# A graph network kernel whose work between the two passes over the edges is cut into chunks of four tiles and dealt out anew to ScalarE, GpSimd and VectorE

## The chip, the cores and the metric

The kernel runs on one core of one Trainium2 chip. The metric is the device time of one execution in microseconds (us), lower is better. The profile's span is the time from the first to the last instruction of one execution; "its own time" is what that same execution took as the metric counts it.

## What is computed

The reference is a two-layer graph network on 6250 nodes of 96 features and 206250 directed edges, sorted by destination. Cut to what matters:

```python
# layer 0
agg_sum = segment_sum(x[src], dst); deg = segment_sum(1, dst)
out1 = batch_norm(x @ W_self1 + (agg_sum / max(deg, 1)) @ W_neigh1, g1, beta1)
hp = relu(x @ W_pool + b_pool)
out2 = batch_norm(x @ W_self2 + segment_max(hp[src], dst) @ W_neigh2, g2, beta2)
x = layernorm(x + leaky_relu(out1 + out2, 0.01))
# layer 1: Q, K, V = x @ W + b; E = edge_attr @ We + be; 8 heads of 12
w = exp(clip(sum_over_head(K[src] * Q[dst] * E / sqrt(12)), -5, 5))
x = layernorm(x + segment_sum(V[src] * w, dst) / (segment_sum(w, dst) + 1e-6))
```

Batch norm takes its mean and variance over all nodes, so nothing behind it can start before the last edge of layer 0 has been summed. Layer 1 gathers rows of K and V at random, so its first gather needs the whole table of them.

## The kernel before, in words

The edges are taken in 404 groups of 512 (four columns of 128), four groups to a turn, 101 turns. Two passes go over all groups.

**Pass 1** (`turn1` on each engine). GpSimd issues four indirect DMAs for each group, which fetch `x[src]` into `kvg` (L469, `gathers`). TensorE transposes the rows (L1194), applies the pool weights (L1205), sums a window of 64 nodes with one-hot matrices (`sums`, L1237), turns the running maximum back (`back`, L1246) and picks the maxima (`ends`, L1254). VectorE makes the one-hot matrices (L742), scans the running maximum (L759) and adds both windows to `acc` (L769: sums in `acc[:, 0]`, maxima in `acc[:, 1]`). The sums, maxima and the features `xT` lie with features on partitions and nodes on columns. Nodes whose edges are all in are finished on the way, in strips of 62 nodes: one strip each turn, `LATE` = 3 turns behind, its linear layers in steps 1 and 3 of the turn, with the batch norm statistics of each strip (L795). The last 174 nodes (`REST`) come after the loop, in order: count (L1297), maximum, reciprocal and product on VectorE (L880 to L884), linear layers (L1299 to L1304), statistics of the rest (L888), then one aggregation over all 99 entries for each branch (L890), square root (L565) and the five small steps that give scale and shift (L896 to L901). Before them each engine loads a flag and branches on it (`irregular`, for inputs whose edges don't fit the strips; not taken here).

**Between the passes** (`nodes`). The 49 tiles of 128 nodes go in seven chunks of seven tiles. For a chunk of 896 columns: ScalarE scales and shifts branch 2 in place (L572); VectorE adds the scaled branch 1 (L927) and takes the leaky ReLU (L930); GpSimd adds `xT` (L487); TensorE transposes to nodes on partitions (L1327); VectorE takes layer norm statistics (L907, L911); ScalarE the square root (L589); VectorE reciprocal and bias (L917, L919); ScalarE normalizes into `xN` (L593); TensorE transposes back (L1319) and ScalarE copies to `xT` (L577); TensorE multiplies with the K and V weights (L1333); VectorE (L936) and ScalarE (L584) copy the table rows to `stage`; SyncE's queue stores them (L367). The engines run the seven chunks skewed by up to three steps. GpSimd then clears `acc[:, 0]` (L490) and all wait until the table is in HBM.

**Pass 2** (`turn2`). GpSimd gathers table rows (again L469, waits for `s_msg` of four groups before); TensorE transposes the edge features and one-hots (L1348, L1355), multiplies with We and spreads the queries (L1364, L1374, L1383) and sums messages (L1391); VectorE multiplies and reduces (L1001, L1012, L1019, L1036); ScalarE copies and takes the exponential (L621, L623, L631). In step 2 of turn 0 TensorE does three extra matmuls that nobody reads (`stay_warm`, L1310). The last 12 turns are written out, with the output rows of finished nodes.

Each engine executes its own instructions in the order written. Between engines there are only counting semaphores. Three lines that the steps below lean on: the second leaky step of the kernel before, what GpSimd does with its result, and the statistics that wait for TensorE:

```python
L930  dve.scalar_tensor_tensor(out=o2, in0=o1, scalar=0.01, in1=o1, op0=ALU.mult, op1=ALU.max)
L487  pool.tensor_tensor(acc[0:D, 0, at], acc[0:D, 1, at], xT[0:D, at], ALU.add)
L907  dve.bn_stats(lnst[:, k, :], source(k))      # source: a bank of PSUM
```

Of the kernel before, what the change touches and what calls it, by code (L numbers as in the profile page):

```python
# [41 lines left out]
KV_BANKS = (6, 7, 4, 5)  # L42
SW = N // TURNS + 1
LATE = 3
# [16 lines left out]
def build(nc, x, src, dst, src_m, src_t, dst_m, dst_t, prv_m, prv_t, nxt_m, nxt_t, edge_attr, Ws1, Wn1, Wp, bp, Ws2, Wn2,  # L61
          g1, be1, g2, be2, Wq, bq, Wk, bk, We, be, Wv, bv, out):
    ctx = ExitStack()
    with ctx:
# [3 lines left out]
        def sem(name):  # L68
# [54 lines left out]
        limit = sb("limit", [1, NS])  # L123
        share = sb("share", [D, W])
        pick = sb("pick", [DSUM, D])
        mv = sb("mv", [D, 2, 2])
# [6 lines left out]
        small = keep[:, :, :].rearrange("p g j -> p (g j)").bitcast(F32)  # L133
        lnst = small[:, 0:K7 * 6].rearrange("p (k c) -> p k c", k=K7)
# [7 lines left out]
        share_rest = prod[0:D, 1, 0:REST]  # L142
        stats = ea[0:D, :, :, :].rearrange("p r j c -> p (r j c)")[:, 0:2 * (NS + 1) * 6].rearrange(
# [8 lines left out]
        early = sb("early", [1, 1])  # L152
# [37 lines left out]
                                                         sem("s_stat"), sem("s_bn"), sem("s_std"))  # L190
        s_countR, s_shareR, s_meanR, s_linR, s_statR, s_copyR = (
# [7 lines left out]
        s_x1T, s_x1c, s_kv, s_kvD, s_kvA = sem("s_x1T"), sem("s_x1c"), sem("s_kv"), sem("s_kvD"), sem("s_kvA")  # L199
# [44 lines left out]
        def pipeline(eng, turn, lag, turns=TURNS, per=R, peel=0, between=(), unrolled=0):  # L244
# [8 lines left out]
            last = turns - unrolled  # L253
# [3 lines left out]
            for p in range(last, turns):  # L257
                turn(p, range(per), lambda r: True)
            turn(turns, range(lag), lambda r: r < 0)

        def node_rows(t, k):

            return bank[t % 2 * 2 + k // 4][:, (k % 4) * D:(k % 4 + 1) * D]
# [20 lines left out]
        def irregular(eng):  # L284

            return eng.If(load_flag(eng) > 0)

# [13 lines left out]
        LAST = ((DONE, DONE + 3), (DONE + 3, NT))  # L301

# [3 lines left out]
        def _(sp):  # L306
# [30 lines left out]
            for w, v, b in ((w_kv[:, 0:D], Wk, bk), (w_kv[:, D:2 * D], Wv, bv),  # L337
                            (w_q[:, :], Wq, bq), (w_e[:, :], We, be)):
                sp.dma_start(w[0:D, :], v[:, :]).then_inc(s_wb, 16)
                sp.dma_start(w[D:D + 1, :], b.rearrange("(a c) -> a c", a=1)).then_inc(s_wb, 16)  # L340
            with nc.allow_non_contiguous_dma(reason="four columns of 96 numbers"):
# [24 lines left out]
            def store_table(i, k0, k1):  # L366
                sp.dma_start(kv_table[bass.ds(i * KC + k0 * P, (k1 - k0) * P), :].rearrange("(t p) c -> p t c", p=P),  # L367
# [1110 lines left out]
```

## Time and profile before

| | us |
|---|---|
| median of 3 runs | 4170.03 (4162.75 to 4170.11) |
| the profiled execution, its own time | 4178.03 |
| its span | 4176.3 |
| busy: TensorE 3767.2, GpSimd 3075.5, VectorE 2324.7, ScalarE 1511.1 | |
| pass 1 ends with the last window added | at 2042.9 |
| batch norm's scale and shift are ready | at 2054.9 |
| the table is in HBM | at 2122.9 |
| first gather of pass 2 | at 2124.0 |

Times "at" are counted from the span's start. "Busy" is the time an engine executed instructions; matmul ends are modelled. In rows of the timeline the first number is the start, the second how long the merged instructions took from first start to last end, and the bracket tells how long the engine had been idle and what ended that.

### The profile page before, as it was taken

What the parts mean: (1) busy time and instruction counts of PE and PEld (TensorE: products, weight loads), DVE (VectorE), ACT (ScalarE), POOL (GpSimd) and SP (SyncE); (2) the same over time, 40 slices, a digit from 0 to 9 for tenths busy, and PEclk for the clock granted to TensorE, in tenths of its full rate; (3) what the DMA queues carried; (4) which work ended last, traced back from release to release, by engine and by line L of the source; (5) the groups of instructions that cost most, each with busy time, mean ns of one, the idle gap of its engine ahead of it and who ended that gap; (6) DMA issues with size and microseconds to landing.
All of it is one profiled execution on the core that took longest, in us unless ns stands there. A gap on an engine that the chain in (4) does not pass through costs nothing.

```text
span 4176.3 us, 105692 instructions
## 1 busy us (share of the span) xinstructions
PE 3767.2 (90%) x30382; PEld 3261.3 (78%) x30382; DVE 2324.7 (56%) x5943; ACT 1511.1 (36%) x4211; POOL 3075.5 (74%) x3246
## 2 busy tenths in 40 slices
PE   7988888888888888888799999999999999999998
PEld 6777777777777777777688888888888888888887
DVE  6555555555555555555545555555555555555666
ACT  3333333333333333333343333333333333333344
POOL 7777777777777777777457777777777777777775
PEclk9999999999999999999779999999999999999998
DMA  3111111111111111111134444444444444444443
GB/s 93 40 40 39 39 40 39 40 40 39 40 40 39 40 39 39 40 39 40 38 108 120 117 118 118 118 119 118 118 118 119 117 118 118 118 118 118 118 121 94
DMA packets 208705, 331.25 MB, mean 79 GB/s; under 512 B 72877, under 2 KB 156520, under 8 KB 208648
## 3 DMA queue, kind: packets, MB, share of 16 engines
q0 software_dynamic: 129040, 238.05, 23.2%
q1 hardware_dynamic: 79608, 92.48, 7.4%
q8 instruction: 30, 0.49, 0.1%
q14 instruction: 27, 0.22, 0.0%
HBM read 323.08 MB, written 7.22 MB: 79 GB/s over the span
## 4 chain that ended last, share of the span: by engine, by line
POOL 42%; issue 32%; PE 12%; DMA 9%; DVE 4%; POOLq 1%; ACT 0%; DVEq 0%; SPq 0%; ACTq 0%
POOL kvg L469 41%; DMA kvg<-kv_table,idx 7%; DMA kvg<-in_x_dram,idx 2%; PE bank L1355 2%; PE bank L1374 1%; PE bank L1194 1%; PE bank L1364 1%; DVE prod L1012 1%; PE bank L1391 1%; DVE msg L1036 1%; PE bank L1205 1%; PE bank L1237 1%; PE bank L1254 1%; PE bank L1348 1%; PE bank L1333 1%
## 5 line engine op out<-in xcount | busy, mean ns | idle before, releaser
L469 POOL DMA_INDIRECT kvg<-kv_table,idx x1613 | 1526.0, 946 | 516.0 <-issue 472.7
L469 POOL DMA_INDIRECT kvg<-in_x_dram,idx x1613 | 1527.2, 947 | 497.2 <-issue 485.9
L759 DVE TENSOR_TENSOR_SCAN scan<-keepC,scan,bank 96x512 f32<-96x512 bf16 x404 | 515.4, 1276 | 495.0 <-PE bank L1205 493.8
L1194 PE MATMUL bank<-ident,kvg 128*96 128x128 f32 x3232 | 450.6, 283 | 228.4 <-DMA kvg<-in_x_dram,idx 218.1
L1194 PEld LDWEIGHTS bank<-ident,kvg 128*96 128x96 f32 x3232 | 365.3, 163 | 293.1 <-DMA kvg<-in_x_dram,idx 218.7
L1355 PE MATMUL bank<-ident,S 128*64 128x128 f32 x3232 | 438.3, 279 | 126.9 <-DVE S L742 124.7
L1001 DVE TENSOR_TENSOR prod<-kvg,bank 128x384 f32<-128x384 f32 x404 | 223.1, 552 | 532.6 <-DMA kvg<-kv_table,idx 393.7
L1355 PEld LDWEIGHTS bank<-ident,S 128*64 128x64 f32 x3232 | 349.0, 138 | 215.7 <-issue 215.7
L1254 PEld LDWEIGHTS bank<-S,scanE 128*96 128x96 f32 x3232 | 338.3, 165 | 216.7 <-issue 214.9
L548 ACT COPY scanE<-bank 128x384 f32<-128x384 f32 x404 | 193.2, 478 | 750.1 <-PE bank L1246 750.1
L1374 PE MATMUL bank<-qwin,scan 64*128 64x96 f32 x3232 | 461.4, 284 | 0.0
L1364 PE MATMUL bank<-w_e,eaC 97*128 97x96 f32 x3232 | 443.1, 281 | 0.0
L769 DVE TENSOR_TENSOR acc<-acc,bank 97x64 f32 (+1 forms) x808 | 177.6, 220 | 469.0 <-issue 461.9
L742 DVE TENSOR_TENSOR S<-bank,rel 128x512 f32<-128x512 f32 (+1 forms) x808 | 435.5, 539 | 2.4 <-DMA kv_table<-stage 2.4
L1205 PE MATMUL bank<-eaC,w_pool 97*96 97x512 f32 x808 | 429.7, 614 | 0.0
L542 ACT COPY eaC<-bank 96x512 f32<-96x512 f32 x404 | 234.9, 581 | 532.5 <-PE bank L1196 532.5
L1374 PEld LDWEIGHTS bank<-qwin,scan 64*128 64x128 f32 x3232 | 394.5, 189 | 39.6 <-issue 1.2
L1364 PEld LDWEIGHTS bank<-w_e,eaC 97*128 97x128 f32 x3232 | 398.6, 194 | 0.8 <-issue 0.8
L621 ACT COPY eaC<-bank 96x512 f32<-96x512 f32 x404 | 234.9, 581 | 437.9 <-PE bank L1348 434.4
L1391 PE MATMUL bank<-S,msg 128*104 128x64 f32 x3232 | 387.4, 264 | 4.3 <-DVE msg L1036 4.3
L1391 PEld LDWEIGHTS bank<-S,msg 128*104 128x104 f32 x3232 | 331.7, 173 | 53.1 <-DVE msg L1036 4.8
L623 ACT COPY scan<-bank 64x512 f32<-64x512 f32 x404 | 233.6, 578 | 325.5 <-PE bank L1355 316.1
(164 smaller groups left out, 5127.2 us busy)
## 6 DMA issues: line engine op xcount, KB each, us to landing
ea<-in_edge_attr_dram SPq DMA_DIRECT2D x402, 192.0 KB
kvg<-in_x_dram,idx POOLq DMA_INDIRECT x1613, 2.5
kvg<-kv_table,idx POOLq DMA_INDIRECT x1613
kv_table<-stage SPq DMA_DIRECT2D x6, 672.0 KB, 3.3
xN<-in_x_dram SPq DMA_DIRECT2D x6, 336.0 KB, 3.2
out_dram<-stage SPq DMA_DIRECT2D x5, 384.0 KB
src_all<-in_src_groups_dram SPq DMA_DIRECT2D x1, 804.0 KB
stage<-in_dst_groups_dram SPq DMA_DIRECT2D x1, 804.0 KB
```

The lines of the kernel that those rows point to most:

```text
L469: pool.indirect_dma_start(out=to[:, r, j, :], out_offset=None, in_=table, in_offset=bass.IndirectOffsetOnAxis(ap=idx[:, r, j:j + 1], axis= ...
L542: act.copy(xeC[0:D, r % 2, :], bank[0][0:D, :])
L621: act.copy(eaC[0:D, r % 2, :], bank[0][0:D, :]).then_inc(s_ec, 1)
L742: dve.tensor_tensor(S[:, r % R, 0:cols * J, :], iota.unsqueeze(1).to_broadcast([P, cols * J, W]), rel[:, bass.ds(i * R + r, 1), 0:cols, :] ...
L759: dve.tensor_tensor_scan(out=scan[:, r % 2, :], data0=keepC[:, r % 2, :], data1=bank[2 + r % 2][0:D, :], initial=scan[:, (r + 1) % 2, GE - ...
L1194: pe.matmul(bank[0][0:D, j:GE:J], xg[:, r, j, 0:D], ident[:, :], start=True, stop=True)
L1205: pe.matmul(bank[2 + b][0:D, :], w_pool[:, :], xeC[:, b, :], start=True, stop=True).then_inc(s_hpT, 1)
L1254: last = pe.matmul(bank[7][0:D, 0:W], scanE[:, b, j, :], S[:, r % R, J + j, :], start=j == 0, stop=j == J - 1)
L1355: last = pe.matmul(bank[1][0:W, j * P:(j + 1) * P], S[:, r % R, j, :], ident[:, :], start=True, stop=True)
L1364: pe.matmul(bank[2 + b][:, j * D:(j + 1) * D], eaC[:, b, j * P:(j + 1) * P], w_e[:, :], start=True, stop=True)
L1374: last = pe.matmul(bank[4 + b][:, j * D:(j + 1) * D], stC[:, b, j * P:(j + 1) * P], qwin[:, b, :], start=True, stop=True)
L1391: last = pe.matmul(bank[6 + b][0:DMSG, 0:W], msg[:, b, j, :], S[:, r % R, j, :], start=j == 0, stop=j == J - 1)
```

## The change

Pass 1: strips come two turns behind in place of three (`LATE` = 2, so the rest is 112 nodes), with mean in step 1 and the linear layers in steps 2 and 3. After turns 98 and 99 VectorE aggregates the first 96 strips' statistics of one branch each and folds the result into one entry (`gathered_stats`). The rest's count, reciprocal and product move into the drain of the pass, ahead of the last two windows of maxima on VectorE, and the flag is loaded there too. The K and V weights are centred by one matmul (`w_kvc`), so that the table can be made from the value before layer norm, scaled by the row's 1/std and with the bias added.

Between the passes: 13 chunks of four tiles (the last has one). ScalarE scales both branches (two activations), GpSimd adds them, VectorE takes the leaky ReLU in place, GpSimd adds `xT`, TensorE transposes and multiplies with `w_kvc` from the same source, VectorE takes the statistics and writes the table rows as scale and bias, ScalarE normalizes into `xN`. The transposes back, the copies to `xT`, ScalarE's table copies and GpSimd's clear are gone from here.

Pass 2: for the first 12 turns (`HEAD`) each step also transposes one tile of `xN` (TensorE), copies it to `xT` (VectorE) and clears one tile of `acc` (ScalarE). `stay_warm` is gone. The first 12 turns are written out on TensorE.

The diff, cut to its core:

```diff
-LATE = 3
+LATE = 2
+NA = TURNS - LATE - 3
+Q = 4
+NQ = -(-NT // Q)
+HEAD = 12
@@ @block.gpsimd @@
+            for k in range(NQ + 1):
+                if k < NQ:
+                    at = columns(k)
+                    pool.wait_ge(s_l, k + 1)
+                    pool.tensor_tensor(acc[0:D, 1, at], acc[0:D, 0, at], acc[0:D, 1, at], ALU.add).then_inc(s_zs, 1)
+                if k >= 1:
+                    at = columns(k - 1)
+                    pool.wait_ge(s_leak, k)
+                    pool.tensor_tensor(acc[0:D, 0, at], acc[0:D, 1, at], xT[0:D, at], ALU.add).then_inc(s_h, 1)
+            pool.wait_ge(s_kvtab, 16 * NQ)
@@ @block.scalar @@
+            for k in range(NQ + 3):
+                if k < NQ:
+                    at = columns(k)
+                    act.activation(acc[0:D, 0, at], acc[0:D, 0, at], ACT.Identity, bias=shs[:, :], scale=ga[:, 0:1])
+                    act.activation(acc[0:D, 1, at], acc[0:D, 1, at], ACT.Copy, scale=ga[:, 1:2]).then_inc(s_l, 1)
+                if 2 <= k < NQ + 2:
+                    t = k - 2
+                    act.wait_ge(s_mv, t + 1)
+                    act.activation(qr[b][:, 0:n], qmv[b].rearrange("p (n c) -> p n c", c=2)[:, 0:n, 1], ACT.Sqrt,
+                                   bias=eps_col[:, 0:1]).then_inc(s_sd, 1)
+                if k >= 3:
+                    t = k - 3
+                    act.wait_ge(s_nb, t + 1)
+                    for j in tiles_of(t):
+                        last = act.activation(xN[:, t * Q + j, :], bank[2 + b][:, j * D:(j + 1) * D], ACT.Identity,
+                                              bias=qb[b][:, j:j + 1], scale=qr[b][:, j:j + 1])
+                    last.then_inc(s_x1, 1)
@@ @block.scalar, turn2 @@
+                def clear_ahead(r):
+                    if head:
+                        clear(act, bass.ds((i * R + r + 1) * P, P))
...
+                def rest_out():
+                    dve.wait_ge(s_countR, 1)
+                    dve.tensor_scalar_max(share_rest, bank[6][0:D, W:W + REST], 1.0).then_inc(s_shareR, 1)
+                    dve.reciprocal(share_rest, share_rest).then_inc(s_shareR, 1)
+                    dve.tensor_tensor(acc[0:D, 0, rest], acc[0:D, 0, rest], share_rest, ALU.mult).then_inc(s_meanR, 1)
...
+            def gathered_stats(m, done, n):
+                part = stats[:, m, NA - 1, :]
+                dve.bn_aggr(mv[:, m, :], stats[:, m, 0:NA, :].rearrange("p n c -> p (n c)")).then_inc(done, 1)
+                dve.memset(part[:, 3:4], float(NA * SW))
+                dve.tensor_copy(part[:, 4:5], mv[:, m, 0:1])
+                dve.tensor_scalar_mul(part[:, 5:6], mv[:, m, 1:2], float(NA * SW)).then_inc(done, 1)
...
-                step(dve.bn_aggr(mv[:, m, :], stats[:, m, :, :].rearrange("p n c -> p (n c)")))
+                step(dve.bn_aggr(mv[:, m, :], stats[:, m, :, :].rearrange("p n c -> p (n c)")[:, NA * 6 - 3:]))
@@ @block.vector @@
+            for k in range(NQ + 3):
+                if k < NQ:
+                    z = acc[0:D, 1, columns(k)]
+                    dve.wait_ge(s_zs, k + 1)
+                    dve.scalar_tensor_tensor(out=z, in0=z, scalar=0.01, in1=z, op0=ALU.mult, op1=ALU.max
+                                             ).then_inc(s_leak, 1)
+                if 2 <= k < NQ + 2:
+                    t = k - 2
+                    dve.wait_ge(s_hN, t + 1)
+                    wait_past(dve, s_x1, t - 1)
...
+                    last.then_inc(s_mv, 1)
+                if k >= 3:
+                    t = k - 3
+                    dve.wait_ge(s_kv, t + 1)
+                    for j in tiles_of(t):
+                        last = dve.scalar_tensor_tensor(
+                            out=stage[:, t * Q + j, :],
+                            in0=bank[4 + t % 2 * 2 + j // 2][:, j % 2 * 2 * D:(j % 2 + 1) * 2 * D],
+                            scalar=qr[t % 2][:, j:j + 1], in1=b_kv[:, :], op0=ALU.mult, op1=ALU.add)
+                    last.then_inc(s_kvD, 1)
+                if 2 <= k < NQ + 2:
+                    t = k - 2
+                    dve.wait_ge(s_sd, t + 1)
+                    dve.reciprocal(qr[b][:, 0:n], qr[b][:, 0:n]).then_inc(s_rs, 1)
@@ @block.tensor @@
+            for t in range(NQ):
+                pe.wait_ge(s_h, t + 1)
+                wait_past(pe, s_x1, t - 1)
+                for j in tiles_of(t):
+                    last = pe.transpose(bank[2 + b][:, j * D:(j + 1) * D],
+                                        acc[0:D, 0, (t * Q + j) * P:(t * Q + j + 1) * P], ident[0:D, 0:D])
+                last.then_inc(s_hN, 1)
+                wait_past(pe, s_kvD, t - 1)
+                for j in tiles_of(t):
+                    last = pe.matmul(bank[4 + b * 2 + j // 2][:, j % 2 * 2 * D:(j % 2 + 1) * 2 * D],
+                                     acc[0:D, 0, (t * Q + j) * P:(t * Q + j + 1) * P], w_kvc[:, :],
+                                     start=True, stop=True)
+                last.then_inc(s_kv, 1)
...
-                        stay_warm(3, 6)
```

## Rows read from the trace of the kernel before

**Rows 1.** The page, costliest groups: GpSimd's gathers of pass 2 (busy, mean ns, idle before).
```profile
L469 POOL DMA_INDIRECT kvg<-kv_table,idx x1613 | 1526.0, 946 | 516.0 <-issue 472.7
```

**Rows 2.** Stretches: us; busy PE, PEld, DVE, ACT, POOL; clock, DMA share, GB/s.
```profile
2060.00:2096.00 36.00, 28.50 (x113) 25.16 (x113) 24.32 (x93) 20.84 (x51) 11.83 (x6) 0.50 0.17 57
...
2123.00:2142.00 19.00, 18.42 (x74) 15.56 (x75) 4.75 (x13) 4.94 (x11) 13.70 (x15) 0.52 0.37 99
2142.00:2162.00 20.00, 20.00 (x162) 17.49 (x161) 10.00 (x29) 7.02 (x25) 13.72 (x15) 1.00 0.39 108
```

**Rows 3.** Timeline of the end of pass 1 and of the batch norm chain.
```profile
2033.29 0.22 DVE L769 TENSOR_TENSOR acc<-acc,bank 96x64 f32 x1 [0.61 <-issue]
...
2040.35 0.66 PE L1246 MATMUL bank<-ident,scan 96*128 96x96 f32 x4
2040.66 0.22 DVE L769 TENSOR_TENSOR acc<-acc,bank 96x64 f32 x1 [1.72 <-PE bank L1254]
...
2042.68 0.22 DVE L769 TENSOR_TENSOR acc<-acc,bank 96x64 f32 x1 [1.80 <-PE bank L1254]
...
2044.30 0.90 PE L1297 MATMUL bank<-acc,pick 97*96 97x174 f32 x2 [1.77 <-issue]
...
2045.61 1.24 DVE L882 RECIPROCAL prod<-prod 96x174 f32<-96x174 f32 x1
...
2050.75 2.83 DVE L890 BATCH_NORM_AGGREGATE mv<-ea 96x2 f32<-96x594 f32 x1
...
2053.67 0.30 ACT L565 ACTIVATE std<-mv,eps_col 96x2 f32<-96x2 f32 x1 [1.32 <-DVEq L891]
...
2054.96 3.18 ACT L572 ACTIVATE acc<-acc,shs,ga 96x896 f32<-96x896 f32 x3 [0.99 <-DVE shs L901]
```

**Rows 4.** Timeline: TensorE's table matmuls of two chunks in a row.
```profile
2079.65 4.85 PE L1333 MATMUL bank<-w_kv,xT 97*128 97x192 f32 x14
...
2087.75 4.85 PE L1333 MATMUL bank<-w_kv,xT 97*128 97x192 f32 x14
```

**Rows 5.** Groups of instructions by form, 2042 to 2124: busy us, mean ns.
```profile
L593 ACT ACTIVATE xN<-bank,keep 128x96 f32<-128x96 f32 x49 | 16.5, 438 | 3.3 <-DVE keep L919 3.3
...
L930 DVE SCALAR_TENSOR_TENSOR acc<-acc 96x896 f32<-96x896 f32 x7 | 9.4, 1338 | 0.2
...
L907 DVE BATCH_NORM_STATS2 keep<-bank 128x6 f32<-128x96 f32 x49 | 8.7, 248 | 0.6 <-PE bank L1327 0.6
...
L572 ACT ACTIVATE acc<-acc,shs,ga 96x896 f32<-96x896 f32 x7 | 7.7, 1131 | 1.0 <-DVE shs L901 1.0
...
L911 DVE BATCH_NORM_AGGREGATE keep<-keep 128x2 f32<-128x6 f32 x49 | 4.0, 154 | 1.0 <-DVE keep L907 0.2
```

**Rows 6.** Timeline around GpSimd's first addition, and a later one.
```profile
2058.40 1.14 DVE L927 SCALAR_TENSOR_TENSOR acc<-acc,ga 96x896 f32<-96x896 f32 x1
2058.87 2.60 POOL L487 TENSOR_TENSOR acc<-acc,xT  x1 [31.69 <-DVE acc L930]
2059.57 2.84 DVE L930 SCALAR_TENSOR_TENSOR acc<-acc 96x896 f32<-96x896 f32 x1
...
2068.35 2.08 POOL L487 TENSOR_TENSOR acc<-acc,xT  x1 [3.51 <-DVE acc L930]
```

**Rows 7.** The chain's piece to the table's landing, and the first gather's timeline row.
```profile
2120.71 2.21 DMA kv_table<-stage
...
2124.04 0.97 POOL L469 DMA_INDIRECT kvg<-kv_table,idx  x1 [16.77 <-issue]
```

**Rows 8.** First groups of pass 2: two TensorE rounds, the extra matmuls, GpSimd's waits.
```profile
2130.69 1.97 PE L1355 MATMUL bank<-ident,S 128*64 128x128 f32 x8
...
2137.83 1.97 PE L1355 MATMUL bank<-ident,S 128*64 128x128 f32 x8
...
2140.05 3.10 PE L1310 MATMUL bank<-xT,ident 96*128 96x448 f32 x6
...
  DVE msg L1036: 3.9, 7
```

More of the change, by code:

```diff
@@ L838, in _ @@
             dve.wait_ge(s_scan, NG + AHEAD)
-            with irregular(dve):
+            with dve.If(held["flag"] > 0):
                 with dve.Fori(0, NCH) as c:
@@ L1187, in _ @@
             pe.wait_ge(s_rel, 1)
+            rest = slice(NS * SW, N)
+            held = {}
             def turn1(i, steps, live):
@@ L1270, in turn1 @@
                         back(r - 2)
+                    if isinstance(i, int) and i == TURNS and r == 1:
+                        pe.wait_ge(s_acc, NG + AHEAD)
+                        pe.matmul(bank[6][0:D, W:W + REST], pick[:, :], acc[0:DSUM, 0, rest], start=True, stop=True
+                                  ).then_inc(s_countR, 1)
+                        held["flag"] = load_flag(pe)
             pipeline(pe, turn1, 3, peel=XTURNS)
-            pe.wait_ge(s_acc, NG + AHEAD)
+            pe.wait_ge(s_xec, NG + AHEAD)
+            pe.wait_ge(s_centre, 1)
+            pe.wait_ge(s_wb, 128)
+            pe.matmul(bank[1][0:D, 0:2 * D], centre, w_kv[0:D, :], start=True, stop=True).then_inc(s_wk, 1)
             pe.wait_ge(s_accm, NG + AHEAD)
-            with irregular(pe):
+            with pe.If(held["flag"] > 0):
+                pe.wait_ge(s_wkc, 1)
+                pe.wait_ge(s_meanR, 1)
                 with pe.Fori(0, NCH) as c:
@@ L1339, in _ @@
[L1339 to L1342 removed]
+                pe.matmul(bank[0][0:D, 0:REST], pick[:, :], acc[0:DSUM, 0, rest], start=True, stop=True
+                          ).then_inc(s_countG, 1)
+                pe.wait_ge(s_meanG, NS + 1)
+            pe.wait_ge(s_meanR, 1)
+            o = bank[6][0:D, R1:R1 + REST]
+            pe.matmul(o, w_self1[:, :], xT[0:D, rest], start=True, stop=False)
+            pe.matmul(o, w_neigh1[:, :], acc[0:D, 0, rest], start=False, stop=True).then_inc(s_linR, 1)
@@ L1343, in transposes, with turn2 @@
+            pe.wait_ge(s_copyR, 2)
+            pe.matmul(bank[0][0:D, 0:P], xN[:, 0, :], ident[:, :], start=True, stop=True).then_inc(s_x1T, 1)
+            pe.wait_ge(s_x1c, 1)
+            pe.wait_ge(s_x1, NQ)
+            pe.wait_ge(s_kvD, NQ)
+            def turn2(i, steps, live, head):
                 def transposes(r):
@@ L1382, in queries @@
                     pe.wait_ge(s_qc, freed(i, r, 2))
+                    if head:
+                        pe.matmul(bank[6 + (r + 1) % 2][0:D, W + P:W + 2 * P],
+                                  xN[:, i * R + r + 1, :], ident[:, :],
+                                  start=True, stop=True)
                     pe.matmul(bank[6 + (r + 1) % 2][0:W, W:W + D], xwin[:, r % 2, :], w_q[:, :], start=True,
```

331 lines of the change are left out of this document (153 added, 178 removed).

## The prediction

> **What bounds the kernel now.** I read the page's groups first. GpSimd's gathers of pass 2 are busy for 1526.0 us and idle before each for 516.0 us in all, nearly all of it its own issue [rows 1]: 2042 us for 1613 gathers, or 5.06 us for a group of four. Pass 1 looks alike. So both passes go at GpSimd's pace, and what a change elsewhere in them saves is hidden; what counts is when the last window of pass 1 is added, when the table lands and how long GpSimd must wait for its first gathers of pass 2. The stretches come second: between the passes TensorE is granted 0.50, its lower level of 1.2 GHz, and the full 2.4 GHz only from about 2142 on [rows 2]. Then the timeline, piece by piece. From the last window at 2042.7 to the first activation of the nodes at 2054.96 runs a chain of small steps [rows 3]; from there to the table's landing at 2120.71 + 2.21 = 2122.92 it is 68.0 us [rows 3, 7]. In that stretch the table matmuls of two chunks start 8.10 us apart [rows 4], that is seven tiles at TensorE's slow pace (79% busy [rows 2]): 1.16 us a tile. The first gather follows the landing by 1.1 us [rows 7], which stays.
>
> **Batch norm chain.** Removed: two aggregations of 2.83 us [rows 3]. In their place stand two over 27 values in place of 594, 0.2 us each in proportion with a small instruction's 0.15 as floor [rows 5]: 5.3 us less. The two long ones go behind turns 98 and 99. They stop VectorE for some 3.1 us each; it is busy for 56% of the span, the gathers run up to four groups ahead, and four groups lie behind the second: 0 to 1 us, I take 0.3. Count, reciprocal and product of the rest move before VectorE's second last window of maxima. The reciprocal of 1.24 us falls to 0.8 for 112 columns; the three make 1.4 us. They can start only when the count matmul, behind the transposes of 2040.35 to 2041.0, is through, at about 2041.3. Then come two register loads (the flag, the window's base) of about 0.6 each [rows 3], so this window, added at 2040.66 before, is added at about 2043.9. TensorE's last picks wait for it (one bank), and the last window falls to 2045.1 in place of 2042.7: 2.4 us later. In return the 1.77 us of flag and branch shrink to some 0.9 (between 0.3, a branch alone, and 1.77), and from the last window to the first activation remain: branch 0.9, two linear layers of 112 columns 1.0, statistics and short aggregates twice 1.2, square root and five small steps 1.29 (2053.67 to 2054.96 [rows 3]): 4.4 us. That gives 2049.5 + 0.3 = 2049.8 against 2054.96. Centring matmul and table load are beside it. I take 5.3 us saved, with ends of 3 and 7.
>
> **The nodes.** Followed by the order on each engine, a ring appears that the kernel before hasn't. ScalarE scales chunk k, then waits for the aggregates of chunk k-2, takes the root, normalizes k-3, and only then scales k+1. VectorE makes the aggregates of k-2 behind its leaky ReLU of chunk k, which waits for GpSimd's sum of k, which waits for ScalarE's scaling of k. So the pace is the sum around the ring, not the busiest engine:
> - two activations of 96x512: a line through 0.438 us at 96 columns and 1.131 at 896 [rows 5] gives 0.80; three in a row took 3.18 [rows 3], an overlap of 0.1 each, and the second has no bias: 1.40 (in proportion to columns alone 1.3);
> - GpSimd's sum: 2.08 for 896 [rows 6], in proportion 1.19, with something fixed 1.22;
> - leaky ReLU: L930's 9.4 us less the one of 2.84 make 1.09 for 896 [rows 5, 6], so 0.69 for 512;
> - four statistics at 8.7/49 and four aggregates at 4.0/49 us [rows 5] and a hand-over: 1.10;
> - root 0.30 [rows 3]; four normalizations at 16.5/49 [rows 5]: 1.35; hand-overs 0.1.
>
> Together 6.1 us for four tiles, 1.54 a tile, against 1.16 now; TensorE's share (four tiles at 4.85/7 [rows 4], 2.8 us, and at most half of that again for transposes) is hidden in it even at the slow clock, and so is GpSimd's second sum. What TensorE's transposes back, the copies and the clear cost is gone but was not on this ring.
>
> There is a second price. GpSimd's first sum began at 2058.87, while VectorE's L927 ran to 2059.54, and took 2.60 in place of 2.08; the L930 that began at 2059.57 took 2.84 in place of 1.09 and ended 0.94 us after GpSimd, at 2062.41 [rows 6]. Each waited for the other: these instructions have two inputs in SBUF. Statistics and copies from PSUM beside GpSimd's later sums show nothing of the kind (L907's mean is 248 ns [rows 5]). In the new order GpSimd starts the `xT` sum of k-1 the moment its sum of k is done, just when the leaky ReLU of k becomes free to start. If GpSimd is there first, the leaky ReLU waits 1.22 us, and the ring is 7.35 us. Bounds: 0 if VectorE is first, 1.22 if never. I take the full price, since the only meeting in the trace was settled so.
>
> The Trainium skill, GPSIMD Engine Reference, Key points, has the rule: GpSimd shares its SBUF interfaces with VectorE, with contention against VectorE instructions that have two SBUF inputs. By it the sum is 9 x 1.22 us and more above that without; the trace agrees (2.84 against 1.09 us). Its Instruction dispatch section adds that a Pool core starts the next instruction as soon as its own share is done, which speaks for GpSimd being first; no row shows it.
>
> Ramps, with the contention: scaling of chunk 3 starts 11.0 us after that of 0 (GpSimd's sums, additions and leaky ReLUs of the first three in turn: 2.7, 0.7, 1.2, 1.2, 0.7, 1.2, 1.2, 0.7, then statistics and root 1.4). Nine rings lead to chunk 12. Behind its start come 5.5 (small chunk, addition of 11, statistics of 10, root, normalization of 9), 3.7 (transposes, statistics, root of 11, normalization of 10) and 2.9 us (transposes, statistics of 12, table rows of 11 and 12), each held by a bank that the normalization frees, then 2.2 for the store [rows 7]. 11.0 + 9 x 7.35 + 14.3 = 91.5 us against 68.0: **23.5 us more**.
>
> **Start of pass 2.** TensorE needs 7.14 us for a group at the slow clock (2130.69 to 2137.83 [rows 8]) against GpSimd's 5.06; GpSimd waited 3.9 us for it in all [rows 8]. Without the extra matmuls, 3.10 us from 2140.05, partly at the slow clock, 1 to 2 us of this go. Each of the 48 head steps gets a transpose, a quarter of L1355's 1.97 us at the slow clock [rows 8], half of that later; hidden behind GpSimd's pace once TensorE has caught up, it costs about 1 us before. VectorE's copy and ScalarE's clear lie in their idle time. Sum -0.7, ends -3.9 (no waits left) and +6 (twelve groups at 0.5).
>
> **Sum.** -5.3 + 23.5 - 0.7 = +17.5. On the profiled execution 4178.03 + 17.5 = 4195.5; that execution stood 8 us above the median of the runs, so against 4170.03 I forecast **4187.5 us**. A measurement here can tell about 0.2%, 8.3 us (the three runs alone spread over 7.4).
>
> **The rivals.**
> - *VectorE is first at the port.* Ring 6.1 us, ramps 8.9 and 13.1: 77 us, +9 in the stretch, +3 in all: 4173. For it: hand-overs between engines are short, and both contenders start within 0.1 us. Against it: [rows 6]. 0.22.
> - *Faster: the ring is not closed*, because a wait that I count comes earlier than I read, and the stretch goes at TensorE's pace of at most 2.8 + 1.4 = 4.2 us a chunk: 22 + 9 x 4.2 = 60 us, -8 - 6 = -14: 4156. The place is ScalarE's wait for the aggregates; it decides below a ring of about 5.8 us, where the sum is zero, and passes the 8.3 us at 4.9. Against it stands the written order on three engines; for it the steps' lengths, estimates all. 0.12.
> - *TensorE stays slow in pass 2.* It is busy for at most 4.2 of 7.35 us before, and nothing fills its gaps any more; ten further groups at 7.14 in place of 5.06 us make +21: 4208. Against it: even now the clock rose at about 2142, 19 us after dense work began [rows 2], with the extra matmuls only in the last two. 0.10.
> - *The drain gains nothing*: the moved steps hold the last windows by more than the aggregates save. It costs 5 us more, 4193, and lies in the forecast's range; 0.06.
>
> The forecast proper keeps 0.50. Faster by over 0.2%: 0.12 and 0.02 from the first rival's edge, 0.14. Within: 0.16 of the first rival, 0.06 of the forecast's edge, 0.22. Slower: the rest, 0.64. The range reaches from the edge of the first rival with a smaller ring (5.8 us), 4166, to 4203, the forecast with the upper ends of its terms; it leaves out the faster rival and most of the slow-clock one.
>
> **What the next profile would show.** The scaling of chunks 3 to 12 starts 7.35 us apart (6.1 if VectorE is first, 4.2 if there is no ring), and ScalarE's idle time there ends on the aggregates. The leaky ReLU shows 1.9 us in place of 0.69, a start beside GpSimd's second sum. The first activation is at about 2049.8, the table lands at about 2141, and GpSimd's waits for messages are 3 us. I am wrong if the landing comes before 2130, or if the time moves after the first gather, where I put nothing but TensorE's start.

## The result, and the profile after

| | before | after |
|---|---|---|
| median (range, runs) | 4170.07 us (4162.75 to 4170.33, 4) | 4190.98 us (4189.30 to 4194.73, 4) |
| ratio | | 1.0062, 95% interval 1.0049 to 1.0075 |
| profiled execution, own time and span | 4178.03, 4176.3 | 4190.33, 4188.5 |
| last gather of pass 1 starts | 2026.2 | 2025.9 |
| first activation of the nodes | 2054.96 | 2051.72 |
| first gather of pass 2 | 2124.04 | 2141.76 |

The change makes the kernel slower by 20.9 us, 17.5 were forecast. The medians are what is compared: the profiled execution of before stood 8 us above its own. First the drain of pass 1, in the timeline of the changed kernel (start, duration, engine, line; idle before in brackets), to be laid beside [rows 3]:

```profile
2042.00 0.58 PE L1356 MATMUL bank<-acc,pick 97*96 97x112 f32 x2
...
2042.92 0.85 DVE L838 RECIPROCAL prod<-prod 96x112 f32<-96x112 f32 x1
...
2045.27 0.22 DVE L805 TENSOR_TENSOR acc<-acc,bank 96x64 f32 x1 [1.19 <-issue]
...
2045.63 1.51 PE L1337 MATMUL bank<-S,scanE 128*96 128x64 f32 x8 [3.05 <-DVE acc L805]
...
2047.30 0.22 DVE L805 TENSOR_TENSOR acc<-acc,bank 96x64 f32 x1 [1.81 <-PE bank L1337]
...
2049.35 0.27 DVE L961 BATCH_NORM_AGGREGATE mv<-ea 96x2 f32<-96x27 f32 x1
...
2051.72 0.81 ACT L613 ACTIVATE acc<-acc,shs,ga 96x512 f32<-96x512 f32 x1 [0.85 <-DVE shs L970]
```

The aggregates have shrunk from 2.83 to 0.27 us, and the last window, in at 2047.30 in place of 2042.68, has taken part of that back. Then one turn of the ring between the passes:

```profile
2083.62 0.81 ACT L613 ACTIVATE acc<-acc,shs,ga 96x512 f32<-96x512 f32 x1
...
2084.33 0.72 ACT L614 ACTIVATE acc<-acc,ga 96x512 f32<-96x512 f32 x1
...
2085.12 1.26 POOL L519 TENSOR_TENSOR acc<-acc 96x512 f32<-96x512 f32 x1 [4.63 <-ACT acc L614]
2086.34 1.26 POOL L523 TENSOR_TENSOR acc<-acc,xT 96x512 f32<-96x512 f32 x1
2086.41 1.73 DVE L997 SCALAR_TENSOR_TENSOR acc<-acc 96x512 f32<-96x512 f32 x1 [2.73 <-POOL acc L519]
2088.07 0.74 DVE L1006 BATCH_NORM_STATS2 keep<-bank 128x6 f32<-128x96 f32 x4
2088.85 0.38 DVE L1010 BATCH_NORM_AGGREGATE keep<-keep 128x2 f32<-128x6 f32 x4
...
2089.26 0.30 ACT L619 ACTIVATE keep<-keep,eps_col 128x4 f32<-128x4 f32 x1 [4.22 <-DVE keep L1010]
2089.47 1.38 ACT L626 ACTIVATE xN<-bank,keep 128x96 f32<-128x96 f32 x4
...
2090.73 0.81 ACT L613 ACTIVATE acc<-acc,shs,ga 96x512 f32<-96x512 f32 x1
```

Each of these rows hangs on the one above it, except L523: it starts at 2086.34, L997 0.07 us later, and L997 takes 1.73 us. From L613 to L613 are 7.11 us. TensorE, busy for 18.3 of 36 us against 28.5 before [rows 2], waits too; it is granted 0.50 all the while:

```profile
2060.00:2096.00 36.00, 18.32 (x64) 15.81 (x62) 22.05 (x77) 13.17 (x31) 12.83 (x11) 0.50 0.13 44
...
2142.00:2160.00 18.00, 18.00 (x75) 14.31 (x73) 3.21 (x10) 3.93 (x11) 13.73 (x15) 0.52 0.36 98
...
2165.00:2350.00 185.00, 185.00 (x1441) 156.03 (x1441) 107.02 (x324) 72.60 (x252) 136.26 (x145) 1.00 0.42 116
```

The last of these stretches is the surprise: in pass 2, at the full clock, TensorE has no gap in 185 us (in the kernel before it was busy for 177.84 of the 185 us from 2147 on). Its timeline there shows a head group of 5.14 us, first row to last:

```profile
2162.68 1.09 PE L1434 MATMUL bank<-ident,S 128*64 128x128 f32 x8
2163.70 0.46 PE L1463 MATMUL bank<-ident,xN 128*96 128x128 f32 x2
...
2167.82 1.09 PE L1434 MATMUL bank<-ident,S 128*64 128x128 f32 x8
```

GpSimd's own pace is four gathers in 5.0 us (1.25 us from start to start). Who waits for whom in the first 260 us of pass 2 tells which engine leads. The gathers of the kernel before (first what GpSimd's idle time ended on, in us and times, then who waited for a gather):

```profile
  issue: 72.8, 185
  DVE msg L1036: 7.9, 20
  ACT idx L522: 0.6, 2
who waited for it (us, times):
  DVE prod L1001: 39.0, 27
```

and of the changed kernel:

```profile
  issue: 67.8, 173
  DVE msg L1117: 8.4, 11
  ACT idx L560: 5.5, 18
who waited for it (us, times):
busy tenths in 40 slices 0000000000000000000037700000000000000000
```

Before, VectorE waited 27 times for a gather: GpSimd led. After, nobody waits for a gather, and GpSimd waits 18 times for indices that ScalarE copies late. 202 gathers start in those 260 us in place of 207, and the 201st starts 258.2 us after the first in place of 251.8.

### The profile page after: what moved, and what is told of

Same layout as the page of the kernel before. It is cut to its first block, busy times and chain, and to the rows that moved or that the text cites. A ratio compares the mean times of both kernels' runs of the same rounds, so it can differ in the third digit from the quotient of the medians.

```text
span 4188.5 us, 106330 instructions
## 1 busy us (share of the span) xinstructions
PE 3779.5 (90%) x30437; PEld 3261.4 (78%) x30437; DVE 2360.5 (56%) x6057; ACT 1525.4 (36%) x4258; POOL 3088.1 (74%) x3265
## 4 chain that ended last, share of the span: by engine, by line
POOL 36%; issue 31%; PE 16%; DMA 10%; DVE 5%; POOLq 1%; ACT 1%; DVEq 0%; SPq 0%; ACTq 0%
POOL kvg L501 35%; DMA kvg<-kv_table,idx 9%; PE bank L1434 3%; PE bank L1453 3%; PE bank L1443 2%; PE bank L1474 2%; DVE prod L1089 2%; DVE msg L1117 1%; DMA kvg<-in_x_dram,idx 1%; PE bank L1427 1%; DVE S L775 1%; PE bank L1466 1%; PE bank L1278 1%; DVE prod L1078 1%; PE bank L1289 0%
## 5 line engine op out<-in xcount | busy, mean ns | idle before, releaser
L1434 PE MATMUL bank<-ident,S 128*64 128x128 f32 x3232 | 437.1, 279 | 109.3 <-DVE S L775 106.5
L1434 PEld LDWEIGHTS bank<-ident,S 128*64 128x64 f32 x3232 | 347.1, 138 | 196.0 <-issue 196.0
L1320 PE MATMUL bank<-S,kvg 128*97 128x64 f32 x3232 | 344.4, 250 | 0.0
```

Source lines behind the costliest of these rows:

```text
L1320: last = pe.matmul(bank[6][0:DSUM, 0:W], xg[:, r, j, :], S[:, r % R, j, :], start=j == 0, stop=j == J - 1)
L1434: last = pe.matmul(bank[1][0:W, j * P:(j + 1) * P], S[:, r % R, j, :], ident[:, :], start=True, stop=True)
```

## The experiments

For the 17.7 us at the first gather the theory is the closed ring, with GpSimd ahead of VectorE's leaky ReLU; against it stands that the smaller chunks are slow for another reason and the order has no part in it. The profile adds a second question: whether the head of pass 2 costs time. All kernels ran beside the kernel before, in three batches in which its median was 4168.58 us (the first four kernels below), 4169.49 (no head to aggregates at the end) and 4168.90 (the last four). Ten executions each stand behind the first four medians, four behind the next three, two behind "aggregates whole", and five to nine behind the rest. With four executions the 95% interval is about 8 us wide to each side, so a saving of 3 to 6 us can't be read from such a median; then the profile is what tells. The ratios carry noise of their own: that of the changed kernel measured again is 1.0053, the quotient of its medians 1.0063.

"Gap" is the time from pass 1's last gather to pass 2's first in the profile, "gathers" how many start in the 260 us from the first on. The finer measure of the same is when the 201st gather starts: the fewer gathers, the later. The expectations count the gathers by adding up three stretches whose borders share some, and so stand up to two too high: their 209 and 210 are 207 and 208 here, their 204 is 202.

**The kernel before again.** 

> The kernel before, unchanged, for a second profile of it. The first profiled execution took 8 us more than the median of its runs and its TensorE fell to 0.50 near 4125 us after a transfer that landed late. If that is an accident of this execution, the new profile shows no such fall or shows it elsewhere, and stands nearer 4170; if it belongs to the kernel, it is there again, and part of the 21 us between the kernels is not between the passes.

Measured: 4164.66 us, ratio 0.9995 (0.9983 to 1.0007). Gap 97.0 (97.8 in the first profile), 208 gathers, the 201st after 250.0 us (251.8). The fall of TensorE's clock at 4124, which lasted 20.5 us, isn't there (granted 1.00 from 4100 to 4140, 0.80 in the first profile), and this execution took 4163.55 us. So the fall belonged to that one execution. How far these two profiles of one kernel differ is the noise of the rest.

**GpSimd's sums swapped.** GpSimd adds `xT` to chunk k-1 before it sums chunk k, so that it is idle when the leaky ReLU comes.

```diff
             for k in range(NQ + 1):
-                if k < NQ:
-                    at = columns(k)
-                    pool.wait_ge(s_l, k + 1)
-                    pool.tensor_tensor(acc[0:D, 1, at], acc[0:D, 0, at], acc[0:D, 1, at], ALU.add).then_inc(s_zs, 1)
                 if k >= 1:
...
                     pool.tensor_tensor(acc[0:D, 0, at], acc[0:D, 1, at], xT[0:D, at], ALU.add).then_inc(s_h, 1)
+                if k < NQ:
+                    at = columns(k)
+                    pool.wait_ge(s_l, k + 1)
+                    pool.tensor_tensor(acc[0:D, 1, at], acc[0:D, 0, at], acc[0:D, 1, at], ALU.add).then_inc(s_zs, 1)
```

> GpSimd adds xT to chunk k-1 before it sums chunk k, in place of behind it; nothing else changes. Ring with port theory: the leaky ReLU no longer meets a GpSimd addition, shows 0.69 us in place of 1.73, and the scalings start 6.05 us apart in place of 7.1; nine rings and the ramps give 10 to 13 us, so 4178 to 4181. Rival (the stretch is set by TensorE at its lower clock, or by the bank that the normalization frees, and the leaky ReLU's length is only a symptom): the spacing stays at 7.1 and the time at 4191.

Measured: 4181.24 us, ratio 1.0030 (1.0018 to 1.0043). In its timeline (L523 is the sum here, L519 the `xT` sum):

```profile
2083.47 1.26 POOL L523 TENSOR_TENSOR acc<-acc 96x512 f32<-96x512 f32 x1 [2.75 <-ACT acc L614]
2084.76 0.69 DVE L997 SCALAR_TENSOR_TENSOR acc<-acc 96x512 f32<-96x512 f32 x1 [2.74 <-POOL acc L523]
2085.53 1.26 POOL L519 TENSOR_TENSOR acc<-acc,xT 96x512 f32<-96x512 f32 x1 [0.80 <-DVE acc L997]
...
2090.83 0.69 DVE L997 SCALAR_TENSOR_TENSOR acc<-acc 96x512 f32<-96x512 f32 x1 [2.74 <-POOL acc L523]
```

The same instruction on the same data takes 0.69 us when GpSimd stands still and 1.73 beside GpSimd's sum. The ring is 6.07 us; nothing but an order changed. The gap falls by 10.5 us, to 105.4, as the theory had it (10 to 13), and the interval of the time lies below the changed kernel's first (1.0049 to 1.0075), though not quite below its second (1.0038 to 1.0068). The order alone does it.

**ScalarE one chunk further ahead.** It scales chunk k+1 where it scaled k, so that the scaling no longer waits for the aggregates of k-2.

```diff
-                if k < NQ:
-                    at = columns(k)
...
+                for c in range(2) if k == 0 else (k + 1,):
+                    if c < NQ:
+                        at = columns(c)
...
```

> ScalarE scales one chunk further ahead (chunks 0 and 1 first, then k+1 in step k), GpSimd's order as in the change. Ring theory: the scaling and GpSimd's sum leave the ring, what is left is the order of VectorE (3.6 us of work a chunk, up to 1.05 more where it meets GpSimd) and TensorE's transposes behind the normalization; scalings 4 to 5 us apart in place of 7.1, 19 to 28 us less, 4163 to 4172. Rival (TensorE or bank sets the pace): under 5 us less. Rival (the port alone is the cost, no ring): the leaky ReLU still takes 1.73 and the spacing falls by under 1 us, under 9 us less.

Measured: 4163.82 us, ratio 0.9989 (0.9978 to 1.0000). In the timeline the leaky ReLUs lie 3.85 us apart:

```profile
2085.52 1.26 POOL L523 TENSOR_TENSOR acc<-acc,xT 96x512 f32<-96x512 f32 x1
...
2086.73 0.68 DVE L998 SCALAR_TENSOR_TENSOR acc<-acc 96x512 f32<-96x512 f32 x1
2086.91 0.88 PE L1404 MATMUL bank<-ident,acc 96*128 96x96 f32 x4 [0.36 <-POOL acc L523]
...
2090.58 0.68 DVE L998 SCALAR_TENSOR_TENSOR acc<-acc 96x512 f32<-96x512 f32 x1
```

The ring is open. A shorter one takes its place (TensorE's transposes, statistics, root, normalization, which frees the transposes' bank), and from the fourth chunk on VectorE gets to the leaky ReLU when GpSimd is done, so it takes 0.68 us without the swap. The row of the transposes names GpSimd as what they waited for, since its sum ends at 2086.78 and the normalization (L627, from 2085.38 for 1.38 us) at 2086.76; the next experiment parts the two. The gap is 84.6 us: 31.3 less than in the changed kernel and 13.2 less than before. But only 4.8 us of this stand in the time; 3.9 us are lost again by the 201st gather of pass 2 (254.8 us after the first, 250.9 in the mean of the kernel before's two profiles).

**Both edits.** 

> Both edits: scaling one chunk ahead, and GpSimd adds xT before it sums the next chunk. Ring with port theory: 4 to 4.5 us a chunk, 24 to 30 us less than the change, 4161 to 4167, so below the kernel before. If the two costs are one and the same wait seen twice, it is no better than the better of the two alone.

Measured: 4167.51 us, ratio 0.9992 (0.9981 to 1.0003); ring 3.84, gap 87.2. Once ScalarE is ahead the swap buys nothing. Here the transposes wait for the normalization alone, at the same pace, so it is their bank that closes the shorter ring:

```profile
2084.32 0.88 PE L1404 MATMUL bank<-ident,acc 96*128 96x96 f32 x4 [0.36 <-ACT xN L627]
```

**No head.** TensorE's transposes of `xN` and VectorE's copies in the first 12 turns of pass 2 are left out (layer 1's queries are then made from the features of before layer 0; ScalarE's clear stays).

```diff
...
-                    if head:
-                        pe.matmul(bank[6 + (r + 1) % 2][0:D, W + P:W + 2 * P],
-                                  xN[:, i * R + r + 1, :], ident[:, :],
-                                  start=True, stop=True)
```

> The change without TensorE's head transposes and VectorE's copies behind them in the first 12 turns of pass 2 (the clear stays; layer 1's queries are then made from x before layer 0's update, so the output is another). In the traces so far GpSimd starts 209 or 210 gathers in the first 260 us of pass 2 in the kernel before and 204 to 206 in all that have the head. If TensorE's 5.14 us a group with the head (4.61 without) is the cause, there are 209 or 210 again, pass 2 is 5 to 7 us shorter and the time about 4185. If the clear, the wait of the window for the queries or the first groups' slow clock is, it stays at 204 to 206 and 4191.

Measured: 4189.68 us, ratio 1.0052 (1.0033 to 1.0071), 207 gathers. Who waits for a gather is as in the kernel before, and TensorE has gaps again (177.71 us busy of 185):

```profile
  issue: 70.2, 191
  DVE msg L1114: 6.3, 12
  ACT idx L560: 1.2, 4
who waited for it (us, times):
  DVE prod L1078: 36.5, 25
```

A group takes 4.61 us in place of 5.14. All five gathers are back, and the 201st starts after 252.5 us, 5.7 earlier than in the changed kernel, though in this execution TensorE stayed at the lower clock until 24.0 us after the first gather, in place of 17.6. So neither the slow first groups alone nor ScalarE's clear, which stayed, cost them. TensorE's transposes and VectorE's copies went together here; that it is the transposes is read from the changed kernel's stretch, where TensorE has no gap and VectorE is busy for 107 of 185 us. In time the 5.7 us are inside the interval.

**A slower head.** One tile every second step over 24 turns; all work is done.

```diff
-HEAD = 12
+HEAD = 24
...
-                    if head:
+                    if head and r % 2 == 0:
...
```

> The change with the head spread over 24 turns, one tile in each second step, and the flag's limit set accordingly. The same work on TensorE, but 4.61 and 5.14 us in turn are 4.9 a group, under GpSimd's 5.0 to 5.06. If what matters is that a group with the head takes longer than GpSimd's pace, the cost of 5 us goes, in the first 260 us 207 to 210 gathers, and the time is near 4186. If it is the amount of work, nothing changes.

Measured: 208 gathers, all of them back, the 201st after 250.7 us; but 4195.03 us, ratio 1.0063 (1.0043 to 1.0084). The interval would hold the changed kernel with 5 us less as well as without. The profiled execution is the longest of the four (4191.16 to 4199.73), and its trace shows where it lost again: from the 401st to the 801st gather it took 504.4 us, 500.0 in the kernel before's second profile, and where that part begins TensorE fell to the lower level for 20.5 us, in which a group took up to 8.5 us:

```profile
2642.00:2663.00 21.00, 20.28 (x92) 18.19 (x93) 7.89 (x23) 4.35 (x15) 15.82 (x18) 0.51 0.36 96
```

What made it fall wasn't tried. Whether the saving reaches the time is told better by the pair with ScalarE ahead, below.

**Count and reciprocal last.** The rest's count, reciprocal and product behind the last window in place of ahead of the last two.

```diff
-                    if isinstance(i, int) and i == TURNS and r == 1:
+                    if isinstance(i, int) and i == TURNS and r == 3:
                         rest_out()
```

> The change with VectorE's count, reciprocal and product of the rest behind the last window of maxima in place of ahead of the second last. If holding the two windows is what made the drain save 3.2 us in place of the 5.3 predicted, the last window is added at about 2044.3 (2047.3 in the change), and the first activation comes at 2050 to 2051 in place of 2051.7. If the place doesn't matter, since the three steps stand on the path either way, it stays at 2051.7 or comes later.

Measured: the first activation comes 23.0 us after the last gather of pass 1 (25.9 in the changed kernel, 28.7 before): 2.8 us better. But picks took 0.89 and 1.06 us, at the higher clock, in place of 1.54 and 1.51: the clock fell 16.9 us after that gather here, and 14.1 us after it in the changed kernel. The other profiles part the two. With the count not moved, the first activation comes after 24.4 to 25.0 us where the clock fell late (16.1 to 19.3 us after the last gather; five versions), and after 25.6 to 26.4 where it fell early (12.6 to 14.7; the changed kernel twice, both edits, slower head). So the place of the count is worth 1.8 us, and the clock 1.1. The time shows neither: 4194.98 us, ratio 1.0070 (1.0050 to 1.0089), from four executions between 4185.85, the profiled one, and 4200.97.

**Aggregates whole, at the end.**

```diff
-                     ending=(lambda: gathered_stats(0, s_part, 0), lambda: gathered_stats(1, s_part, 2), lambda: None))
+                     ending=(lambda: None, lambda: None, lambda: None))
...
-                step(dve.bn_aggr(mv[:, m, :], stats[:, m, :, :].rearrange("p n c -> p (n c)")[:, NA * 6 - 3:]))
+                step(dve.bn_aggr(mv[:, m, :], stats[:, m, :, :].rearrange("p n c -> p (n c)")))
```

> The change with both aggregations whole at the end, over all entries, and nothing folded in turns 98 and 99. By the sum the first activation comes 2 x (2.83 - 0.27) = 5.1 us later, at 2056.8, less what the long instructions cost the pass where they stand now (0.3 us as predicted). If they cost the drain 2 us, it comes only 3 us later, at 2054.8, and TensorE's picks there run before its clock falls.

Measured: 4197.01 us, ratio 1.0071 (1.0046 to 1.0096). Two aggregates of 2.86 us, first activation 30.4 us after the last gather, 4.5 later than in the changed kernel, with the clock falling at the same place (14.1 us after that gather). The aggregates inside the pass are worth 4.5 of their 5.2 us.

**The changed kernel again.** 

> The changed kernel once more, unaltered, for a second profile and more times beside the others. Both theories: 4190 us, ratio 1.005; leaky ReLU 1.73 us, ring 7.1 us, 204 gathers started in the first 260 us of pass 2. If one of these moves, the comparison with it in the other experiments has to be read with that spread.

Measured: 4195.36 us, ratio 1.0053 (1.0038 to 1.0068); leaky ReLU 1.73 us, gap 115.7, 202 gathers, the 201st after 258.5 us.

**Extra matmuls put back.**

```diff
+                    if isinstance(i, int) and i == 0 and r == 2:
+                        pe.wait_ge(s_qc, ready(0, 1))
+                        for _ in range(3):
+                            pe.matmul(bank[6][:, 0:CH], ident[0:D, :], flat[0:D, 0:CH], start=True, stop=True)
```

> The changed kernel with the three extra matmuls in step 2 of turn 0 put back (they took 3.10 us in the kernel before). If the missing extra matmuls are why TensorE stays at 1.2 GHz for longer in pass 2, the clock rises at least one group (8 us) earlier and one gather is won, 1 to 2 us of time. If they only take TensorE's time, which is the bound there, the clock rises where it did (about 18 us after the first gather) and the first 260 us hold 203 or 204 gathers; 4190 to 4193 us, ratio 1.005.

Measured: 4195.41 us, ratio 1.0058 (1.0044 to 1.0073), 203 gathers. The clock did rise 7 us earlier, but ahead of the extra matmuls, not behind them:

```profile
2148.84 1.97 PE L1434 MATMUL bank<-ident,S 128*64 128x128 f32 x8
...
2154.62 1.09 PE L1434 MATMUL bank<-ident,S 128*64 128x128 f32 x8
...
2156.33 2.52 PE L1487 MATMUL bank<-stage,ident 96*128 96x448 f32 x6
```

So this kernel says nothing for the extra matmuls as a means to raise the clock. It does give their price: its 201st gather starts after 257.3 us, and after 254.6 to 255.0 in the four kernels with the full head, without them, whose clock rose as early. The 2.3 to 2.7 us between are the 2.52 us of L1487: what was put on TensorE there was paid in full.

**ScalarE ahead and the slower head.** 

> The same without the moved count: ScalarE one chunk ahead and the slow head. If the savings add up, 3 us more than the version with all three edits, 4159; if pass 2 gives them back, 4164 for both.

Measured: **4156.35 us, ratio 0.9967 (0.9954 to 0.9981)**: faster than both kernels. Gap 84.6, 208 gathers, and VectorE waits for gathers again:

```profile
  issue: 70.6, 189
  DVE msg L1118: 4.9, 16
  ACT idx L560: 0.9, 3
who waited for it (us, times):
  DVE prod L1079: 16.0, 19
```

The 201st gather starts after 250.1 us, 4.7 earlier than with ScalarE ahead and the full head. Against that kernel the ratio is less by 0.0022, or 9 us, but the two were measured in different batches, and the intervals just touch (that one's begins at 0.9978). So the saving is clear in the gathers, and in the time it is likely and not shown.

**All three.** 

> Three edits at once: ScalarE scales one chunk further ahead, the head takes one tile every second step over 24 turns, and the rest's count, reciprocal and product stand behind the last window. If the three savings (12.8 us, 5 us, 2.7 us, all measured relative to the gathers) add up and pass 2 keeps them, the change of 20 us becomes none: 4190.5 - 20.5 = 4170 by the changed kernel, but the lead alone was measured at 4163.8, so from there 4163.8 - 7.7 = 4156, ratio 0.996 to 0.997. If pass 2 gives back what comes earlier, as it seemed to with the slow head alone, 4164, ratio 0.9985 to 1.000. First gather about 15 us earlier relative to pass 1's last gather than in the changed kernel, 208 to 210 gathers in its first 260 us.

Measured: 4160.35 us, ratio 0.9979 (0.9967 to 0.9990), 205 gathers, the 201st after 254.1 us, since the clock rose only 25.4 us after the first. The first gather comes 32.0 us earlier than in the changed kernel (gap 83.9 for 115.9), not 15: the expectation had taken the lead for 12.8 us, which is its gain against the kernel before. The first activation comes 24.1 us after the last gather, 0.7 earlier than in the kernel without the moved count, because the picks fell into the lower clock here (13.7 us after the last gather) and not there (16.3); against the four profiles with a fall as early it is 1.8 us. The intervals of the last two kernels overlap.

**Two sums over all versions.** The first: what the gap and the time to the 201st gather are above the kernel before's (97.4 and 250.9 us, the means of its two profiles), beside the measured difference of medians in the same batch.

| | gap | gathers | 201st after | sum | measured |
|---|---|---|---|---|---|
| the change | 115.9 | 202 | 258.2 | +25.8 | +20.9 |
| again | 115.7 | 202 | 258.5 | +25.9 | +26.5 |
| extra matmuls | 114.5 | 203 | 257.3 | +23.4 | +26.5 |
| swapped sums | 105.4 | 205 | 255.0 | +12.1 | +12.7 |
| ScalarE ahead | 84.6 | 205 | 254.8 | -8.9 | -4.8 |
| both | 87.2 | 202 | 258.2 | -3.0 | -1.1 |
| no head | 115.0 | 207 | 252.5 | +19.2 | +20.2 |
| slower head | 116.0 | 208 | 250.7 | +18.5 | +25.5 |
| count last | 113.1 | 205 | 254.6 | +19.4 | +25.5 |
| aggregates at the end | 120.4 | 205 | 254.6 | +26.8 | +27.5 |
| ahead, slower head | 84.6 | 208 | 250.1 | -13.6 | -12.6 |
| all three | 83.9 | 205 | 254.1 | -10.3 | -8.6 |

Seven of the twelve agree within 2 us and one within 3.1; the change, ScalarE ahead, the slower head and the count last are 4 to 7 us off, in both directions. The sum is from one execution each and leaves out what lies behind the 201st gather, where two profiles of one kernel differ by as much (last section). The second sum parts the two causes of late gathers, the head and the time until TensorE's clock rises (counted from the first gather). The entries are the times of the 201st gather:

| clock rises after | no head, or the slower one | full head |
|---|---|---|
| 9.5 to 10.7 us | 250.0, 250.1, 250.7 | 254.6, 254.6, 254.8, 255.0; 257.3 with the extra matmuls |
| 17.2 to 18.4 us | 251.8 | 258.2, 258.2, 258.5 |
| 24.0 to 25.4 us | 252.5, 254.1 | |

The head costs 4 to 5 us with the early rise and 6.4 to 6.7 with the later one; 8 us more at the lower clock cost 1 to 2 us without it and 3 to 4 with it. With the head on it TensorE can't catch up what the slow groups cost.

## Why the prediction was right, and which term was wrong

**The batch norm chain, forecast 5.3 us less: 3.2.** The aggregates in the pass, the branch and the small steps came as reckoned. The last two windows did not. The step put them at 2043.9 and 2045.1; they came at 2045.27 and 2047.30. It had taken TensorE at the full clock in the drain. The picks took 1.54 and 1.51 us where they take 0.89 to 1.06 at the higher level, so the count matmul came 0.7 us late and the last window 2.2. In part the 3.2 is a matter of which executions were profiled: the clock fell 16.1 us after the last gather in the kernel before and 14.1 in the changed one. Compared at a like fall, early with early and late with late, the first activation comes 3.5 and 3.9 us sooner.

**The nodes, forecast 23.5 more: 20.9** (88.9 us from first activation to landing, 68.0 before). The shape is as written, all three pieces: chunk 3 is scaled 10.6 us after chunk 0 (11.0 forecast), nine rings take 63.9 (66.2), and 14.4 lead to the landing (14.3). From start to start the ring of 7.11 us is scaling 1.50 (forecast 1.40), sum 1.29 (1.22), leaky ReLU with contention 1.66 (1.91), statistics and aggregates 1.19 (1.10), root and normalization 1.47 (1.75 with the hand-overs). The contention was priced too high: GpSimd's whole 1.22 us was added to the 0.69, but L997's end follows GpSimd's by 0.54 us (2088.14 against 2087.60). That stood in [rows 6] already, where L930 ended 0.94 after GpSimd and not 1.09. Swapping the sums showed the price alone: 7.11 less 6.07, 1.04 us a ring.

The Trainium skill, SBUF — State Buffer, section "SBUF: two separate sides", says that the shared ports are locked for a whole instruction and that the other engine blocks fully. By it L997 would do none of its 0.69 us before L523 ends; the trace agrees but for 0.15 us, the 0.54 in place of 0.69 just named.

**The start of pass 2, forecast 0.7 less: 6.4 more** (the 201st gather after 258.2 us in place of 251.8). This is the step that failed: "hidden behind GpSimd's pace once TensorE has caught up". A head step was priced at 0.25 us at the full clock and is 0.53 (5.14 less 4.61): L1463's two matmuls alone show 0.46, where a quarter of L1434's eight would be 0.27. At 0.25 a group would have been 4.86, under GpSimd's 5.0, and TensorE would have caught up by 0.14 us a group. At 5.14 it never does: the delay from the first slow groups stays and grows by 0.14 a group for 48 groups, 6.7 us, less what the four groups of lead absorb. The gathers show it: from the 51st to the 201st they take 193.0 us in place of 187.5, 0.15 a group, and behind the head, from the 201st on, 62.5 for 50 as before. The upper end of that term (+6) comes near it, but it was argued with the wrong reason, the slow clock. The prediction named as a sign of being wrong that the time moves after the first gather, where it put nothing but TensorE's start. By that sign this part of it was wrong: 6.4 us moved there, and in the first 260 us GpSimd waited 8.4 us for messages where 3 were forecast.

**The sum.** -3.2 + 20.9 + 6.4 is +24.1, between the two measured differences of 20.9 and 26.5; the forecast of +17.5 was short by the head, and the two other misses, 2.1 and 2.6, cancel. That they cancel is luck, and so in part is the nearness of 4187.5 to 4190.98: the same kernel measured again stood 26.5 us above the kernel before.

Some of the working doesn't add up as written, by little: the ring's terms make 6.16 and 7.38 us, not 6.1 and 7.35 (0.3 us over nine rings), and the chain 2054.96 - 2049.8 = 5.2, not 5.3. The range is looser than its own terms: a ring of 5.8 us gives a sum of zero, 4170 and not 4166, and the upper ends of the terms, -3, +23.5 and +6, give 4196.5 and not 4203. The measured time lies inside the narrower range too.

**The rivals.** VectorE first at the port: no, but the swap made it so, with a ring of 6.07 us where the rival said 6.1. The ring not closed: no, but one chunk of lead opened it, with 3.85 us where 4.2 was the bound. TensorE slow in pass 2: the clock rose 17.6 us after the first gather, 17.2 before, so not in these two; the drain gaining nothing: no, 3.2. What the runs add is that the late clock doesn't hang on the ring: with the ring closed it rose between 9.6 and 24.0 us after the first gather, with the ring open between 10.2 and 25.4.

## What to carry to other kernels

Add up a software pipeline around each loop that the written orders close, not by the busiest engine: here four engines of which none was busy for more than 61% (22.05 of 36 us) gave 7.11 us a chunk, and one chunk of lead on one engine brought 3.85. Where VectorE reads two SBUF operands, look at what GpSimd starts in the same moment, and order it so that it doesn't. And work that is moved under the cover of the leading engine must fit in the difference of the two paces: between 4.61 and 5.0 us there was room for 0.39 and not for 0.53, and with the same 48 tiles spread over 96 groups no gather was lost in the two profiles whose clock rose early. The third, whose clock rose last of all, had three gathers fewer.

## What was unexpected

TensorE's clock in pass 2 rose 9.5 to 10.7 us after the first gather in eight of the fourteen profiles, 17.2 to 18.4 in four and 24.0 and 25.4 in two, though in all fourteen TensorE was busy without a gap (9.00 of 9.00, then 15.50 of 15.50 us) from 0.5 to 25 us after that gather. The kernel before alone had 17.2 in one execution and 9.5 in the other. So from one profile each the moment of the rise can't be put down to an edit, and an experiment on it needs several; one look at a pair of them would have credited the extra matmuls with 7 us.

The time after the first 260 us of pass 2, where all versions do the same, differs from profile to profile: from first to last gather it was 2024.3 and 2016.3 us for the kernel before, and 2024.9 and 2030.0 for the changed one. Of the kernel before's 8.0 us, 1.7 lie ahead of the 201st gather and 6.4 behind the 1501st, where the first profile has TensorE at the lower level from 3994.7 to 4015.2 and from 4124.4 to 4144.9, and the second never. The own times go with the clock too: of the 31 executions of the kernel before in the first batch, the five shortest (4158 to 4161 us) were granted 0.986 to 0.988 over the whole execution, the five longest (4175 to 4177 us) 0.981 to 0.983. Whether the clock is cause or sign, and what makes it fall, wasn't tried.
